# A row quantiser in another order of columns: block scales side by side, bf16 product, clip behind the rounding

## What is computed

```python
def fake_quant_nvfp4(x, global_scale):
    xb = x.reshape(sh[:-1] + (sh[-1] // BLOCK, BLOCK))          # BLOCK = 16
    amax = jnp.max(jnp.abs(xb), axis=-1, keepdims=True)
    sc = jnp.clip(amax / FP4_MAX * global_scale, 0.0, FP8_MAX)  # 6.0, 448.0
    sc8 = sc.astype(jnp.float8_e4m3fn).astype(jnp.float32)
    dq = sc8 / global_scale
    a = jnp.clip(jnp.abs(xb) / safe_dq, 0.0, FP4_MAX)
    q = jnp.sign(xb) * _FP4_VALS[jnp.digitize(a, _FP4_MIDS)]
    return (q * dq).reshape(sh)

def nvfp4_linear(x, w, s_in):      # both operands quantised, then a matrix product
    return jnp.einsum('bsh,oh->bso', fake_quant_nvfp4(x, s_in), fake_quant_nvfp4(w, s_w))

x = x + gnn(layernorm(x)) + mix(layernorm(x))
h = layernorm(x)
hidden = silu(nvfp4_linear(h, gate_w, s_in)) * nvfp4_linear(h, up_w, s_in)
x = x + nvfp4_linear(hidden, down_w, s_in_down)
```

## Time and profile before

| what | value |
|---|---|
| runs | 1056.94, 1059.74, 1411.92 us; median 1059.74 |
| profiled execution | 1058.53 us, of which span 1056.8 us |
| PE busy | 959.5 us, 91% of the span |
| DVE busy | 837.9 us, 79% |
| ACT busy | 648.7 us, 61% |
| POOL busy | 496.7 us, 47% |
| granted TensorE clock, mean | 0.967 |
| the chain that ended last | PE 15%, DVE 7% of the span, issue 1% |

### The profile page before, as it was taken

The page is one execution under the profiler, slowest core; times in us unless marked ns, Lnnn a source line. Parts: engine busy times, 40 slices in busy tenths (PEclk is TensorE's granted clock), DMA queues, the critical chain, the costliest instruction groups (busy, mean ns, idle before and its releaser), DMA issues. The chain is left out here.

```text
span 1056.8 us, 17499 instructions
## 1 busy us (share of the span) xinstructions
PE 959.5 (91%) x5429; PEld 794.3 (75%) x5429; DVE 837.9 (79%) x1395; ACT 648.7 (61%) x1435; POOL 496.7 (47%) x582
## 2 busy tenths in 40 slices
PE   2698879999999999999997779999999879999986
PEld 2676779999999999999997357888898334454443
DVE  5875567888888888888888868998995768887776
ACT  3274446665765766666664568999898335554442
POOL 0211777777777777777771524444444200110000
PEclk9699889999999999999998899999999989999998
DMA  9304588989889898998872689989985364674314
GB/s 246 56 7 110 169 243 259 292 265 280 257 254 294 266 287 284 288 280 282 277 244 91 247 198 332 293 278 310 290 270 192 79 135 122 149 160 112 81 19 79
DMA packets 109977, 221.40 MB, mean 209 GB/s; under 512 B 25883, under 2 KB 58228, under 8 KB 109857
## 3 DMA queue, kind: packets, MB, share of 16 engines
q1 hardware_dynamic: 89053, 159.98, 47.2%
q0 software_dynamic: 20576, 60.08, 23.8%
q10 hardware_dynamic: 260, 0.20, 0.1%
HBM read 156.56 MB, written 62.95 MB: 208 GB/s over the span
## 5 line engine op out<-in xcount | busy, mean ns | idle before, releaser
L1024 POOL DMA_INDIRECT score_gath<-xl_rows,misc x324 | 347.4, 1072 | 101.6 <-issue 92.1
L1064 PE MATMUL score_ps_m<-x_hi,score_w_hi 128*128 128x416 f32 (+1 forms) x576 | 209.4, 363 | 2.1 <-DVE score_w_lo L1217 1.9
L1065 PE MATMUL score_ps_m<-x_lo,score_w_hi 128*128 128x416 f32 (+1 forms) x576 | 204.1, 354 | 0.0
L1066 PE MATMUL score_ps_m<-x_hi,score_w_lo 128*128 128x416 f32 (+1 forms) x576 | 204.1, 354 | 0.0
L1784 ACT ACTIVATE agg_gath<-agg_gath,prob 128x64 f32<-128x64 f32 x648 | 159.2, 353 | 6.7 <-DMA agg_gath<-edge_rows 6.4
L1196 DVE TENSOR_TENSOR score_zb<-score_gath,score_ps_x 128x1024 f32<-128x1024 f32 x81 | 98.8, 1219 | 67.6 <-PE score_ps_x L1047 57.9
L1733 PE MATMUL ps_all<-agg_gath,agg_hot 128*125 128x128 f32 x648 | 128.0, 280 | 9.8 <-DVE agg_hot L1839 6.4
L1735 PE MATMUL ps_all<-agg_gath,agg_hot 128*125 128x136 f32 x648 | 128.9, 281 | 0.0
L1733 PEld LDWEIGHTS ps_all<-agg_gath,agg_hot 128*125 128x125 f32 x648 | 100.5, 189 | 25.8 <-issue 25.2
L2081 PE MATMUL ps_all<-mix_w,phi_c 128*125 128x512 f32 x240 | 108.4, 602 | 5.8 <-DVEq L2355 5.2
L1064 PEld LDWEIGHTS score_ps_m<-x_hi,score_w_hi 128*128 128x128 f32 x576 | 109.7, 190 | 4.2 <-issue 2.6
(11 more groups left out here) (341 smaller groups left out, 1666.3 us busy)
## 6 DMA issues: line engine op xcount, KB each, us to landing
edge_rows<-score_gath SPq DMA_DIRECT2D x81, 528.0 KB, 3.8
agg_gath<-edge_rows SPq DMA_DIRECT2D x81, 528.0 KB, 5.6
local_bc<-local_rows SPq DMA_DIRECT2D x40, 224.0 KB
score_gath<-xl_rows,misc POOLq DMA_INDIRECT x324, 4.5
phi_c<-phi_rows SPq DMA_DIRECT2D x10, 500.0 KB, 6.1
x_bo<-in_x SPq DMA_DIRECT2D x10, 500.0 KB
x_bo<-in_L_mix_bo POOLq DMA_DIRECT2D x10, 500.0 KB, 7.2
out<-fin_x SPq DMA_DIRECT2D x9, 500.0 KB
```

Source lines behind the costliest of these rows:

```text
L1024: nc.gpsimd.indirect_dma_start(out=gath[:, g % GS, q, :], out_offset=None, in_=xl_rows, in_offset=bass.IndirectOffsetOnAxis(ap=src_idx[:, ...
L1064: pe.matmul(acc, w_hi[:, i % 2, kk, :], x_hi[:, kk, cols], start=(kk == 0), stop=False)
L1065: pe.matmul(acc, w_hi[:, i % 2, kk, :], x_lo[:, kk, cols], start=False, stop=False)
L1066: mm = pe.matmul(acc, w_lo[:, i % 2, kk, :], x_hi[:, kk, cols], start=False, stop=(kk == KC - 1))
```

## The change

The order of the columns in h, hidden and their quantised tiles changes, by blocks of 512: where before column 16n + s stood at its place, it now stands at 32s + n (n the block of 16, 0 to 31, s the place in it). So values of different blocks lie side by side, and the scales of 32 blocks lie beside each other too, repeated for each s. Two functions, `by_lane` and `natural`, give the walks through such tiles.

- ACT's `normalise` and DVE's `hidden` read in the old order and write in the new one; the largest of a block is taken by a reduction that reads 16 values 32 elements apart.
- The weights' product in `aggregate` writes its bf16 output in the new order, so `gate_q` and `down_q` fit.
- `scaled` and `product` read their scale row with the repetition in the middle (32 neighbours, 16 times over); before, each scale was repeated 16 times at once.
- The scale row sc8 is kept in bf16, the second rounding instruction writes bf16 (into coarse), the clip follows it there in place, and the product has bf16 on both inputs and its output.
- The clip ahead of the sizes is gone: the sizes and the rounding see values that aren't clipped.

```diff
--- before.py
+++ after.py
@@ -1532,6 +1532,19 @@
                 q.wait()
 
 
+LANES = 32
+
+
+def by_lane(ap):
+
+    return ap.rearrange("p (b s n) -> p b n s", s=16, n=LANES)
+
+
+def natural(ap):
+
+    return ap.rearrange("p (b n s) -> p b n s", s=16, n=LANES)
+
+
 NEAR_ONE = 1.0 + 2.0 ** -7
 COARSE = NEAR_ONE * 2.0 ** 22
 
@@ -1579,7 +1592,8 @@
 
     def product(self, out, j):
 
-        return self.v.tensor_tensor(self.blocks(out), self.blocks(self.work), self.wide(0, j), ALU.mult)
+        scale = self.small[:, 0, j * self.nb:(j + 1) * self.nb].rearrange("p (b n) -> p b n", n=LANES)
+        return self.v.tensor_tensor(by_lane(out), natural(self.work), scale.unsqueeze(3).to_broadcast([P, 2, LANES, 16]), ALU.mult)
 
 
 def aggregate(nc, a, k):
@@ -1875,29 +1889,33 @@
     def __init__(self, v, steps, amax, small, work, coarse):
         self.v, self.q, self.amax, self.small, self.work, self.coarse = v, steps, amax, small, work, coarse
 
+    def wide(self, row, width):
+
+        return row.rearrange("p (b n) -> p b n", n=LANES).unsqueeze(2).to_broadcast([C, width // 512, 16, LANES])
+
+    def scale_row(self, width):
+
+        return self.small[0:C, 2, :].bitcast(BF16)[:, 0:width // 16]
+
     def scales(self, x, width):
 
         v, q = self.v, self.q
         nb = width // 16
         amax = self.amax[0:C, 0:nb]
-        t, sc8, inv = (self.small[0:C, i, 0:nb] for i in (0, 2, 3))
+        t, inv, sc8 = self.small[0:C, 0, 0:nb], self.small[0:C, 3, 0:nb], self.scale_row(width)
         p2 = self.small[0:C, 1, :].bitcast(BF16)[:, 0:nb]
-        q.do(v.tensor_reduce(amax, x.rearrange("p (n s) -> p n s", s=16), AX.X, ALU.max, apply_absolute_value=True))
+        q.do(v.tensor_reduce(amax.rearrange("p (b n) -> p b n", n=LANES), by_lane(x), AX.X, ALU.max, apply_absolute_value=True))
         q.do(v.tensor_scalar(t, amax, (1.0 - 2.0 ** -22) / 6.0, 448.0, ALU.mult, ALU.min))
         q.do(v.tensor_scalar(p2, t, NEAR_ONE * 2.0 ** -6, 2.0 ** 20, ALU.max, ALU.mult))
-        q.do(v.tensor_tensor(sc8, t, p2, ALU.add))
-        q.do(v.tensor_tensor(sc8, sc8, p2, ALU.subtract))
+        q.do(v.tensor_tensor(inv, t, p2, ALU.add))
+        q.do(v.tensor_tensor(sc8, inv, p2, ALU.subtract))
         q.do(v.tensor_scalar(t, sc8, 2.0 ** -20, -1.0, ALU.max, ALU.mult))
         q.do(v.reciprocal(inv, t))
 
-    def clipped(self, x, width):
-
-        v, q = self.v, self.q
-        nb = width // 16
-        a = self.work[0:C, 0:width]
-        blocks = lambda ap: ap.rearrange("p (n s) -> p n s", s=16)
-        q.do(v.tensor_tensor(blocks(a), blocks(x), self.small[0:C, 3, 0:nb].unsqueeze(2).to_broadcast([C, nb, 16]), ALU.mult))
-        q.do(v.tensor_scalar(a, a, 6.0, -6.0, ALU.min, ALU.max))
+    def scaled(self, x, width):
+
+        lanes = lambda ap: ap.rearrange("p (b s n) -> p b s n", s=16, n=LANES)
+        self.q.do(self.v.tensor_tensor(lanes(self.work[0:C, 0:width]), lanes(x), self.wide(self.small[0:C, 3, 0:width // 16], width), ALU.mult))
 
     def sizes(self, width):
 
@@ -1909,14 +1927,13 @@
 
         v, q, a, b = self.v, self.q, self.work[0:C, 0:width], self.coarse[0:C, 0:width]
         q.do(v.scalar_tensor_tensor(out=a, in0=b, scalar=COARSE, in1=a, op0=ALU.max, op1=ALU.add))
-        q.do(v.scalar_tensor_tensor(out=a, in0=b, scalar=COARSE, in1=a, op0=ALU.max, op1=ALU.subtract))
+        q.do(v.scalar_tensor_tensor(out=b, in0=b, scalar=COARSE, in1=a, op0=ALU.max, op1=ALU.subtract))
+        q.do(v.tensor_scalar(b, b, 6.0, -6.0, ALU.min, ALU.max))
 
     def product(self, out, width):
 
-        nb = width // 16
-        return self.v.tensor_tensor(out.rearrange("p (n s) -> p n s", s=16),
-                                    self.work[0:C, 0:width].rearrange("p (n s) -> p n s", s=16),
-                                    self.small[0:C, 2, 0:nb].unsqueeze(2).to_broadcast([C, nb, 16]), ALU.mult)
+        lanes = lambda ap: ap.rearrange("p (b s n) -> p b s n", s=16, n=LANES)
+        return self.v.tensor_tensor(lanes(out), lanes(self.coarse[0:C, 0:width]), self.wide(self.scale_row(width), width), ALU.mult)
 
 
 def finish(nc, a, k, out):
@@ -2232,7 +2249,7 @@
 
                 def normalise(c):
                     act.wait_ge(s_scale, c + 1)
-                    act.activation(h, x1[:, c % 3, :], ACT.Identity, bias=shift, scale=rstd).then_inc(s_h, 1)
+                    act.activation(by_lane(h), natural(x1[:, c % 3, :]), ACT.Identity, bias=shift, scale=rstd).then_inc(s_h, 1)
 
                 def copy_gnn(c):
                     act.wait_ge(s_gt, c + 1)
@@ -2369,7 +2386,7 @@
                 def clip_x(b):
                     v.wait_ge(s_h, b + 1)
                     quant_x.scales(h, D)
-                    quant_x.clipped(h, D)
+                    quant_x.scaled(h, D)
                     v.sem_inc(s_clip_x, 1)
 
                 def round_x(b):
@@ -2383,12 +2400,12 @@
                 def hidden(b):
                     v.wait_ge(s_e, b + 1)
                     v.wait_ge(s_g, b + 1)
-                    own.do(v.scalar_tensor_tensor(out=hid[:, :], in0=ps_g[0:C, 1, :], scalar=fs[0:C, 6:7], in1=e[:, :],
-                                                  op0=ALU.mult, op1=ALU.mult))
+                    own.do(v.scalar_tensor_tensor(out=by_lane(hid[:, :]), in0=natural(ps_g[0:C, 1, :]), scalar=fs[0:C, 6:7],
+                                                  in1=natural(e[:, :]), op0=ALU.mult, op1=ALU.mult))
                     v.sem_inc(s_hid, 1)
 
                 def clip_h(b):
-                    quant_h.clipped(hid[:, :], FF)
+                    quant_h.scaled(hid[:, :], FF)
                     v.sem_inc(s_clip_h, 1)
 
                 def round_h(b):
```

## The result

The changed kernel takes 1096.76 us (median; 1093.29 to 1099.97), the kernel before, beside it, 1058.82: a ratio of 1.036, 95% interval 1.032 to 1.041. One of the four executions of the kernel before took 1411.92 us, as in the table of times before; the ratio is worked out without it. The change makes the kernel slower by 38 us. The forecast was +13.5 us, 1072 us; its range ended at 1088.

The account below looks back on a forecast made before the run. It took all engines as near their limit in the aggregation, and DVE, then PE, then DVE as bounding the last stage. Turns 6.66, head 1.03, end 2.95 and aggregation 2.9 made +13.5 us: 1072 us, range 1054 to 1088.

Parts of the forecast that it names:

- Aggregation:* each product +1.07 on DVE: Aggregation: each weights' product 1.07 us longer on DVE, partly covered by waits and PE's lag, +2.9 us in all.
- I take the scan's two cycles: All SBUF streams stepping 32 elements: 2.08 ns an element on DVE, +1.07 us for 1024, +0.53 for 512.
- zsum's 2.8 ns: Upper bound for a hop's price, from the slowest elementwise row (L780), 878 ns for 256 elements.
- 4.6 us of waits: Aggregation, 640 to 747 us: DVE's waits of 4.1 + 0.5 us, taken to absorb part of seven longer products.
- PE's lag of 4.8: End of aggregation: PE starts the last group 4.8 us after DVE's last one-hot; the last four products' 4.3 us fit in.
- 6.66 + 1.03 + 2.95: Last stage: +6.66 us for the loop's turns, +1.03 for the head, +2.95 for the end after the last residual.
- a turn: Last stage, one loop pass over chunks, from one `hidden` to the next: +2.10 us, 20.95 us in place of 18.85.
- The head: Last stage, chunks 0 and 1: copy_x stands behind ACT's later sizes, +1.03 us for the gates of chunk 0.
- the 0.35 of its rounding: Head, chunk 0: round_x ends 0.35 us later, its rounding starting 0.42 later with no clip ahead.
- The product stays at one element a cycle: Rival, last stage: broadcast scale keeps the bf16 product slow, +0.80 us a turn, 1077 us; chance 0.10.
- Hops are free: Rival: every SBUF stream hops at full rate, as the PSUM row does; -3.6 us, 1055 us; chance 0.16.
- Hops are much dearer: Rival: 2.8 ns for each hop; turns +18.7, head +4.8, end +6.7, aggregation +8.0; +38, 1097 us; chance 0.21.

Follow-up runs that it names:

- agg_only: Kernel before, with only the weights' product storing in the new order: 1093.7 us beside 1060.53, ratio 1.0325.
- probe: Kernel before, with single DVE and ACT instructions on scratch memory behind its last store: two-byte product hopping 32 elements 4.6 us, whole-kernel time not given.
- pairs: Changed kernel, with two neighbouring elements of a block kept side by side so every hop follows a pair: 1057.83 us beside 1060.29 of before, ratio 0.9987.

## Why the prediction was wrong, step by step

**The step that failed** is the price in "*Aggregation:* each product +1.07 on DVE". It came from "I take the scan's two cycles", one price for every stream that steps 32 elements, read from a row of four-byte elements. The weights' product stores two-byte elements, and measured +3.46 us each, (4672 - 160) / 1024 = 4.4 ns an element. I had said that the stream was "1024 bf16, twelve times" and then costed it as if that made no difference. Worse for the range: the upper bound, zsum's 2.8 ns, was again a four-byte row, and so no bound for this one. Nor does the scan or zsum hop at all: both walk neighbours and are slow for some other reason. That the scan's 2.08 ns came near what a hop of four bytes costs (1.71, below) was luck.

**The accounting around that step came out, in part by luck.** By the same sum with 3.46 us: 7 x 3.46 less the 4.6 us of waits is 19.6, 4 x 3.46 less PE's lag of 4.8 is 9.0, together 28.7. The sum left out the first of the twelve, at 627 us; with its 3.46 us it gives 32.1. Measured: 32.5 in the trace, 33.2 by `agg_only`. What held is that DVE's longer product comes first out of time in which DVE waits, and that the rest arrives. The time to spare, 9.4 us in the sum, was 41.5 - 32.5 = 9.0 in this execution and some 8.5 by the medians, but it is made up otherwise: over the whole stage DVE's waits for edge rows fell from 13.8 to 5.5 us, 8.3 where I counted 4.6 up to 747 us, and of PE's lag 0.7 us were used up and not 4.8. The last four products did not fit into that lag; the two errors nearly cancel.

**The last stage** I put at 6.66 + 1.03 + 2.95 = +10.6; it cost +7.0. Up to the last residual it was +4.6 for the foretold 7.7, behind it +2.4 for 2.95. Mis-sized here was the hop of four bytes, in the other direction. Between 512 and 1024 elements the reductions differ by 1925 - 1050 ns, so 1.71 ns an element and not 2.08. With the measured durations my own steps give a turn of 0.36 + 0.36 + 0.94 - 0.03 + 0.70 - 0.85 = +1.48, and it measured +1.56 (20.39 for 18.83; my 18.85 was a slip of 0.02). The order of events was as told: DVE waits for normalise and PE for xq in four turns, and the last three stay PE's. PE's first wait for xq was 1.65 us, where I had said more than 3. The head cost nothing (-0.3 in place of +1.03). Chunk 0 arrives as before: the residual of chunk 1 starts 31.45 us after the start of the stage (880.20), and 31.44 before (847.69), so the 0.35 of its rounding did not arise. In chunk 1 PE reached the first transposes of xq 0.6 us earlier, since ten matmuls ahead of them took 6.01 us (881.54) in this execution and 6.61 in that of before (849.04); PE had been idle for 4.98 us ahead of them in both, and the granted clock around them was 0.77 (881.5 to 888 us) and 0.70 (849 to 856 us), so that in the execution of before more of this stretch ran at the lower of the clock's two levels, 1.2 GHz. Without that the head would have cost some 0.3 us, by an estimate from these rows.

The Trainium skill, "Vector Engine (DVE) Microarchitecture Reference", section 5.2, which I cited against the change, had the four-byte price right for an instruction with two sources and for the reductions: 1.71 to 1.76 ns, which the trace agrees with (1.71 by the reductions, and (1886 - 160) / 1024 = 1.69 by the product of `probe`). The TENSOR_SCALAR of `probe` pays less, 1135 ns for 1024 elements. The section's 2.50, given for a step of 24 words, isn't what a step of 32 words costs here. For a store of two bytes it has no figure. Its rule that runs of two adjacent words of four bytes stream at the full rate is what `pairs` rests on, and the trace agrees: 693 ns for 512 elements in the scaling of x. That a pair of two-byte elements, a single word, is enough (689 ns in the weights' product) the section doesn't state; the runs show it.

**What became cheaper** came as read from the rows: xq's product 0.69 us, the clips 0.43 and 0.29, and hq's product 0.43; as single lines:

```profile
L1936 DVE TENSOR_TENSOR misc<-parts,fin_small x10: 691/693/694, 879.3 to 1071.4; 125x1024 bf16<-125x1024 bf16 x10
L1936 DVE TENSOR_TENSOR fin_hq<-prob,fin_hid_small x10: 424/426/426, 918.0 to 1087.5; 125x512 bf16<-125x512 bf16 x10
L1931 DVE TENSOR_SCALAR parts<-parts x10: 426/427/507, 878.8 to 1070.9; 125x1024 bf16<-125x1024 bf16 x10
L1931 DVE TENSOR_SCALAR prob<-prob x10: 293/293/295, 917.7 to 1087.0; 125x512 bf16<-125x512 bf16 x10
```

**The rivals.** "The product stays at one element a cycle" is out by these lines; the broadcast in the middle does no harm, but one innermost would have (1227 ns against 691 in `probe`). The Trainium skill, "Vector Engine (DVE) Microarchitecture Reference", section 5.1, has one element read 16 times by an instruction with two sources and two-byte operands at one element a cycle, and the trace agrees. "Hops are free" is out for single elements; for pairs it holds, and there its -3.6 us measured -2.5 by the medians and -1.4 by the ratio, with an interval from -3.3 to +0.5. "Hops are much dearer" named 1097 us, which is the time measured, but by luck and not for its reason: it had 2.8 ns for every hop, +18.7 us in the turns and +8.0 in the aggregation, where it was +4.6 and +32.5.

## What to carry to other kernels

When a layout is changed, cost each stream of it by element size, direction and step, and look for a row of just that kind; where there is none, the bound from another kind is not a bound, and a probe behind the kernel's end settles it in one run. Where two neighbours stayed side by side, the hops of this case ran at the full rate (`pairs`, 0.69 us for 512 elements). And before a stage near its limit on all engines is given work for the sake of another, compare the time it has to spare (here some 8.5 us) with the whole count of instructions.

## What the runs showed of the hardware that was not expected

- A product that stores 1024 two-byte elements 32 elements apart takes 4.6 us with nothing else running, 4.4 ns an element; stored as four bytes, 1.89 us. With a TENSOR_SCALAR the two are 2.51 and 1.14 us. In both, a two-byte store that hops alone takes a little over twice as long as a four-byte one. Why the product pays more than the TENSOR_SCALAR in either case wasn't tested.
- The two-byte price of a TENSOR_SCALAR builds up with the step: 0.76 us at 2 elements, 1.32 at 4, 2.44 at 8, 2.51 at 32.
- ACT pays as well. A copy of 1024 elements to bf16, 32 elements apart, takes 4.76 us (L2297, while DVE ran too); with a load that hops it takes 2.03 (L2301), and the changed kernel's normalise, a four-byte store, 2.18 where it was 1.24.

```profile
L2297 ACT ACTIVATE parts<-fin_y 125x1024 bf16<-125x1024 f32 x1 | 4.8, 4763 | 0.0
L2301 ACT ACTIVATE parts<-fin_y 125x1024 bf16<-125x1024 f32 x1 | 2.0, 2027 | 0.0
```
